# Routing tokens through DRAM to their two experts in a recurrent + mixture-of-experts kernel

## Chip, core and metric

One core of one Trainium2 chip runs the whole program. The metric is device time in microseconds of one launch, as the median of three runs.

## What is computed (reference, cut)

```python
# x: (2, 2048, 256) fp32; 4096 tokens
xB = einsum('bsd,nd->bsn', x, B)                    # n = 128 states
state = tanh(state @ A.T + xB[:, t])                # for t in 0..2047, in order
y = states @ C.T + D * x + x
x = layernorm(x + layernorm(y) * gamma + beta)
scores = sigmoid(x @ router_weight.T)               # 8 experts in 2 groups of 4
# choose the better group, in it the top 2 experts; weights normalised to sum 1
g, u = x @ w_gate[e], x @ w_up[e]                   # 256 -> 128, for each expert
routed = sum_e comb[t, e] * ((silu(g) * u) @ w_down[e])
shared = (silu(x @ sw_gate) * (x @ sw_up)) @ sw_down
out = layernorm(x + routed + shared)
```

Only two of the eight entries of `comb` are not zero for a token. The reference computes all eight experts.

## The kernel before, in words

The sequence is cut into 128 chunks of 32 tokens, one chunk to a partition; a tile `l` (0 to 31) holds the l-th token of every chunk. The scan therefore has 32 serial steps for all chunks together. A first pass of 4 + 32 steps (`WARM` = 4) finds the state at which each chunk starts; a second pass of 32 steps from these seeds writes `states`. At the end of the second pass `met` compares the seeds with the last states; if they differ by more than 2^-20, a serial path is taken. Each scan step is a `BT` product issued ahead (`drive`), an `AT` product (L298) and a tanh on ScalarE (L512).

While the first pass runs, x and the weights are loaded by SyncE. VectorE takes each weight's largest absolute value (L620), scales it and splits it in two fp16 halves, high and low (`split`, L647 and L649). An fp32 product is made of three fp16 products: high*high, high*low, low*high. GpSimd prepares `xskip` = x*(1+D) (L918, eight times) and x+beta (L926, eight times).

After the scan the tokens are worked in 8 groups of 4 tiles (512 tokens). For each group g all 9 experts (8 routed and the shared one) follow one another. For an expert: 12 fp16 products of 512 columns for gate and up (`up_products`, L371), a silu on ScalarE (L554), a product on VectorE (L827), for a routed expert a second one with its column of `comb` (L831), a high half on ScalarE (L565), a low half on GpSimd (L961), and 12 fp16 products of 256 columns for down (`down_product`, L439). The columns of `comb` are written to DRAM (L236) and read back spread over all partitions (L241, 8 loads of 256 KB a group).

Between the experts of group g, `piece(e, g + 1, ...)` does the front part of group g+1: C product (L333 or L338), statistics (L675, L680), gamma (L699), residual (L706), second normalisation (L715), transposes on TensorE (L348), their halves (L494, L721), logits (L359), and `choose` and `weigh` (L740 to L786). GpSimd does the inverse square roots (`rsqrt`, L942 and L944). The order on every engine is written out by hand in `group`; `Fori` loops over pairs of groups.

## Time and profile before

| | |
|---|---|
| median of 3 runs | 424.69 us (422.93 to 426.33) |
| profiled execution, span | 423.6 us |
| between its span and the median of the runs | 1.1 us |
| TensorE busy (matmul) | 378.8 us, 89% |
| VectorE busy | 323.5 us, 76% |
| GpSimd busy | 163.7 us, 39% |
| ScalarE busy | 138.0 us, 33% |
| DMA | 29.95 MB, 71 GB/s over the span |

The scan ends at 95.3 us, the groups' experts run from 98 to 416 us, and the rest is the last normalisation and the last store. A busy engine is not by itself the bound: which wait ends last in a stage has to be read there. Times are from the start of the span.

### The profile page before, as it was taken

To read this page: it belongs to the slowest core of one execution; us is meant where nothing else is said; L and a number is where in the kernel's file an instruction comes from. 1 tells how busy PE (TensorE), PEld (TensorE's weight loads), DVE (VectorE), ACT (ScalarE), POOL (GpSimd) and SP (SyncE) were. 2 spreads that over 40 slices of the span, in tenths; PEclk is the share of its full clock that TensorE was granted. 3 is DMA by queue.
4 is the path that set the end of the run, shared out by engine and by line. 5 is a ranking of instruction groups with operands and counts; after the bars stand their busy time and mean duration, and the time that the engine had idled before them with its cause. 6 is when DMAs were issued, how large, how long until landed. Compare 5 with 4: busy or idle time off the path is not lost.

```text
span 423.6 us, 7485 instructions
## 1 busy us (share of the span) xinstructions
PE 378.8 (89%) x2583; PEld 254.6 (60%) x2583; DVE 323.5 (76%) x740; ACT 138.0 (33%) x280; POOL 163.7 (39%) x151
## 2 busy tenths in 40 slices
PE   6899529596999998999899999999998999899992
PEld 5899428582566665666556556655565565565561
DVE  2343998445587699979978997999699969984464
ACT  2454102132233423242433244233432342333330
POOL 1870697300442334235423542344244234514242
PEclk9999958699899999999999999999999999999997
DMA  7980000003800460153018211901260145016311
GB/s 187 315 300 2 0 0 2 0 2 63 140 2 0 86 117 2 52 123 79 7 47 152 49 52 34 158 8 50 68 132 0 50 109 93 0 53 141 59 52 50
DMA packets 15901, 29.95 MB, mean 71 GB/s; under 512 B 1720, under 2 KB 4288, under 8 KB 15872
## 3 DMA queue, kind: packets, MB, share of 16 engines
q1 hardware_dynamic: 15872, 29.58, 29.9%
q8 instruction: 17, 0.28, 0.3%
q14 instruction: 12, 0.10, 0.1%
HBM read 25.24 MB, written 4.33 MB: 70 GB/s over the span
## 4 chain that ended last, share of the span: by engine, by line
issue 28%; PE 22%; POOL 18%; DVE 18%; DMA 5%; SPq 5%; ACT 2%; POOLq 1%; DVEq 0%; ACTq 0%
PE bank L371 11%; POOL h L961 9%; PE bank L439 4%; POOL xres L926 4%; DVE st L675 3%; SPq L205 3%; POOL rstd L944 3%; DVE wu L706 3%; DVE xT L827 3%; DMA xT<-comb_dram 2%; PE bank L292 2%; DVE xT L831 2%; DVE wg L715 2%; DMA xres<-in_L_attn_x_dram 2%; PE bank L298 1%
## 5 line engine op out<-in xcount | busy, mean ns | idle before, releaser
L961 POOL TENSOR_TENSOR h<-xT,h 128x512 f16<-128x512 f32 x72 | 86.2, 1198 | 185.8 <-ACT h L565 177.0
L439 PE MATMUL bank<-wd,h 128*128 128x256 f16 x864 | 106.9, 274 | 5.6 <-POOL h L961 4.9
L371 PE MATMUL bank<-x2T,wg 128*128 128x512 f16 x432 | 105.3, 379 | 0.0
L371 PE MATMUL bank<-x2T,wu 128*128 128x512 f16 x432 | 105.3, 379 | 0.0
L439 PEld LDWEIGHTS bank<-wd,h 128*128 128x128 f16 x864 | 84.4, 98 | 30.5 <-POOL h L961 5.7
L565 ACT ACTIVATE h<-xT 128x512 f16<-128x512 f32 x72 | 45.3, 630 | 131.7 <-DVE xT L831 128.2
L371 PEld LDWEIGHTS bank<-x2T,wu 128*128 128x128 f16 x432 | 42.3, 98 | 50.3
L827 DVE SCALAR_TENSOR_TENSOR xT<-bank,u_un,xT 128x512 f32<-128x512 f32 x64 | 47.6, 744 | 23.1 <-ACT xT L554 22.2
L554 ACT ACTIVATE xT<-bank,g_un 128x512 f32<-128x512 f32 x72 | 49.2, 683 | 43.2 <-PE bank L371 40.4
L371 PEld LDWEIGHTS bank<-x2T,wg 128*128 128x128 f16 x432 | 41.8, 98 | 35.6 <-issue 0.3
L831 DVE TENSOR_TENSOR xT<-xT 128x512 f32<-128x512 f32 x64 | 44.3, 692 | 8.4 <-DMA xT<-comb_dram 6.5
L292 PE MATMUL bank<-xT,BT 128*128 128x128 f32 x272 | 44.7, 290 | 0.0
L292 PEld LDWEIGHTS bank<-xT,BT 128*128 128x128 f32 x272 | 38.9, 206 | 0.1
L944 POOL TENSOR_TENSOR rstd<-rstd,neghalf 128x4 f32<-128x4 f32 (+1 forms) x25 | 25.6, 1025 | 2.0
L918 POOL TENSOR_TENSOR xskip<-xres,D_bc 128x1024 f32<-128x1024 f32 x8 | 20.5, 2586 | 10.3 <-issue 7.3
L675 DVE BATCH_NORM_STATS2 st<-wu 128x6 f32<-128x256 f32 x64 | 23.3, 416 | 0.8
L512 ACT ACTIVATE states<-bank 128x128 f32<-128x128 f32 x32 | 8.9, 278 | 42.2 <-PE bank L298 42.2
L706 DVE SCALAR_TENSOR_TENSOR wu<-wu,rstd,xres 128x256 f32<-128x256 f32 x32 | 21.7, 742 | 1.0 <-POOL rstd L944 1.0
L926 POOL TENSOR_TENSOR xres<-xres,beta_bc 128x1024 f32<-128x1024 f32 x8 | 22.3, 2815 | 0.0
L348 PE MATMUL bank<-ident,wg 128*128 128x128 f32 x64 | 11.2, 294 | 12.4 <-DVE wg L715 7.7
L715 DVE TENSOR_SCALAR wg<-wu,mv,rstd 128x256 f32<-128x256 f32 x32 | 19.7, 679 | 1.7 <-POOL rstd L944 1.4
L333 PE MATMUL bank<-CT,states 128*128 128x256 f32 x16 | 6.4, 516 | 13.0 <-DVE wu L690 13.0
(114 smaller groups left out, 356.8 us busy)
## 6 DMA issues: line engine op xcount, KB each, us to landing
xT<-comb_dram SPq DMA_DIRECT2D x64, 256.0 KB, 7.5
xres<-in_L_attn_x_dram SPq DMA_DIRECT2D x7, 512.0 KB, 5.9
out_dram<-xskip SPq DMA_DIRECT2D x7, 512.0 KB, 2.7
wd<-in_L_ffn_w_down_dram SPq DMA_DIRECT2D x1, 1024.0 KB, 7.0
xres<-in_L_attn_x_dram SPq DMA_DIRECT2D x2, 256.0 KB, 3.4
out_dram<-xskip SPq DMA_DIRECT2D x2, 256.0 KB, 2.0
B_sb<-in_L_attn_B_dram SPq DMA_DIRECT2D x1, 128.0 KB, 2.2
C_sb<-in_L_attn_C_dram SPq DMA_DIRECT2D x1, 128.0 KB
```

The lines of the kernel that those rows point to most:

```text
L292: pe.matmul(ps_scan[s % 2][:, 0:P], BT[:, k, :], xT[:, k, tile, :], start=(k == 0), stop=False)
L371: last = pe.matmul(ps[:, :], w[:, pw, e, m // 3, :], x2T[:, par, px, m // 3, :], start=(m == 0), stop=(m == NUP // 2 - 1))
L439: return pe.matmul(ps_y[t // 2][:, (t % 2) * DM:(t % 2 + 1) * DM], h16[:, e % 3, ph, t * P:(t + 1) * P], wd16[:, pw, e, :], start=start, s ...
L554: nc.scalar.activation(sg[:, b, :], ps_g[b][:, :], ACT.Silu, scale=g_un[:, 0:1]).then_inc(silu_done, 1)
L565: nc.scalar.activation(h16[:, e % 3, 0, :], h[:, b, :], ACT.Copy).then_inc(h_high, 1)
L675: nc.vector.bn_stats(st[:, k, t, :], src(t)).then_inc(st_sem, 1)
L706: nc.vector.scalar_tensor_tensor(y1[:, t, :], y1[:, t, :], rstd[:, 0, 1, t:t + 1], xres[:, g * T4 + t, :], ALU.mult, ALU.add).then_inc(sem ...
L827: nc.vector.scalar_tensor_tensor(gu[:, b, :], ps_u[b][:, :], u_un[:, 0:1], sg[:, b, :], ALU.mult, ALU.mult).then_inc(gu_done, 1)
L831: nc.vector.tensor_tensor(h[:, b, :], comb_all[:, e - 1, :], gu[:, b, :], ALU.mult).then_inc(h_done, 1)
L926: nc.gpsimd.tensor_tensor(xres[:, c * T4:(c + 1) * T4, :], xres[:, c * T4:(c + 1) * T4, :], beta_bc[:, :].unsqueeze(1).to_broadcast([P, T4 ...
L944: nc.gpsimd.tensor_tensor(rstd[:, k, 1, t0:t1], rstd[:, k, 0, t0:t1], neghalf[:, t0:t1], ALU.pow).then_inc(ready, 1)
L961: nc.gpsimd.tensor_tensor(h16[:, e % 3, 1, :], h[:, b, :], h16[:, e % 3, 0, :], ALU.subtract).then_inc(h_low, 1)
```

## The change

- The first scan pass has 32 steps instead of 36. Loads are reordered (the down weights last). The greatest weights are combined over partitions by two small TensorE steps instead of GpSimd. Only gate, up and router weights are split; `wd` and `C` stay fp32, and their products are single fp32 products.
- Normalised tokens are kept as fp16 high and low halves, one row of 1 KB for each token (`rows16`), and are transposed by TensorE as fp16.
- After the choice of experts (`choose`, now with `max` and `max_index` for each tile), TensorE ranks each token within its expert by products with a triangle and with ones (`ranks`), VectorE turns ranks into row numbers (`slots`), and GpSimd writes the rows to DRAM, sorted by expert, by 8 indirect DMAs of 128 rows for each group (`scatter`), 64 in all.
- The groups are in two parts, 0 to 4 and 5 to 7 (`PARTS`). At the end of a part `count`, `table` and `back` make lists of tiles of 256 rows, and SyncE fills the unused rows (`pad`, 9 DMAs). There are always 27 tiles in part 0 and 19 in part 1.
- A tile is one routed job: a DMA transpose of 256 rows of 1 KB from DRAM (`load_tile`), 12 fp16 products of 256 columns with the weights of an expert read from a table, silu, one product on VectorE, 2 fp32 products for down, a copy by ScalarE (`keep_y`) and a store to DRAM. 16 jobs of 256 tokens do the shared expert. That makes 62 jobs.
- At the end, for each pair of tiles u (16 pairs), GpSimd reads each token's two rows back by 4 indirect DMAs (`gather`), VectorE adds them with their weights (`combine`), GpSimd makes the inverse root (4 small instructions), and ScalarE normalises (`finish`). Pairs 0 to 9 belong to part 0 and stand between the routed jobs of part 1.
- The path for seeds that were not met is a serial one at the end of the program.
- The order on all engines comes from one list of tokens (`PLAN`), fully unrolled.

```diff
-    WARM = 4
+    PARTS = ((0, 5), (5, 8))
+    SLOTS = 2 * P
+    JT = [TK * (g1 - g0) * GT // SLOTS + E - 1 for g0, g1 in PARTS]
+    RING = 4
+    LAG = 2
+        def period(p, jobs, spread):       # p: group in front, g: group routed
+            g = p - 1
+            if p > 2:
+                if p < G:
+                    put(("A", p))
+                put(("X", g, 0), ("X", g, 1))
+                some(spread[0])
+                if p < G:
+                    put(("S", p))
+            put(("Y", g, 0), ("Y", g, 1))
...
+            put(("T", g, 0))
+            some(spread[1])
+            put(("T", g, 1))
+            if p > 2 and p < G:
+                put(("B", p))
+            some(spread[2])
...
+            put(("L", g))
+            some(spread[3])
+            put(("D", g))
+            some(spread[4])
+            put(("P", g))
+            some(spread[5])
+            put(("E", g))
+            if g + 1 == PARTS[part_of[g]][1]:
+                put(("N", part_of[g]))
...
+        period(5, shared(3), (0, 1, 0, 1, 0, 0))
+        period(6, shared(4) + shared(5)[:0] + ra[:5], (1, 1, 1, 1, 1, 2))
+        period(7, ra[5:13], (1, 2, 1, 2, 1, 1))
+        period(8, ra[13:20], (1, 1, 1, 2, 1, 1))
+        for what in ra[20:] + shared(5):
+            job(*what)
...
+            def load_tile(h, j):                                   # SyncE
+                row = sp.value_load(tabR[0:1, h, j:j + 1], min_val=0, max_val=E * CAP[h])
+                sp.dma_start_transpose(xjob[:, r % RING, :, :], xs_dram[h][bass.ds(row, SLOTS), :]).then_inc(xjob_in[r % RING], 16)
...
+            def up(n):                                             # TensorE
+                    pe.wait_ge(xjob_in[r % RING], 16 * (r // RING + 1))
+                    e = pe.value_load(tabE[0:1, p, j:j + 1], min_val=0, max_val=E)
...
+            def scatter(g):                                        # GpSimd
+                pool.wait_ge(slots_ready, g + 1)
+                pool.wait_ge(x2_low, 2 * g + 2)
+                for t in range(g * T4, (g + 1) * T4):
+                    for r in range(TK):
+                        nc.gpsimd.indirect_dma_start(out=xs_dram[hp], out_offset=...)
+            def gather(u):
+                if u >= 2:
+                    pool.wait_ge(comb_step, 4 * (u - 1))
+                for t in range(2):
+                    for r in range(TK):
+                        nc.gpsimd.indirect_dma_start(out=yback[:, u % 2, t, r, :], out_offset=None, in_=ys_dram[hp], ...)
```

In `PLAN` the letters are: A the C product and first statistics, S gamma, B residual and second statistics, X the second normalisation and high half, Y the low half, T transposes, L logits, D choice, P ranks, E slots and scatter, N the tables of a part, J a job, G gather, Z combine, R inverse root, W finish and store.

## Rows read from the trace of the kernel before

**Rows 1.** Stretch, us; busy of PE, PEld, DVE, ACT, POOL; clock, DMA share, GB/s.
```profile
98.50:415.50 317.00, 303.76 (x2037) 186.91 (x2036) 262.21 (x632) 108.16 (x178) 113.39 (x114) 0.99 0.31 66
183.00:223.07 40.07, 38.92 (x267) 24.09 (x266) 35.69 (x88) 13.86 (x23) 14.71 (x15) 1.00 0.26 67
```
**Rows 2.** The chain that ended last: some of TensorE's pieces (start, us, what).
```profile
109.13 1.71 PE bank L333 x4
...
127.72 2.59 PE bank L371 x12
130.31 1.31 PE bank L439 x12
```
**Rows 3.** Timeline of the scan (start, us, engine, line, [idle before, releaser]).
```profile
42.75 0.28 ACT L518 ACTIVATE seed<-bank 128x126 f32<-128x126 f32 x1 [0.58 <-PE bank L298]
...
60.95 1.22 PE L333 MATMUL bank<-CT,states 128*128 128x256 f32 x2 [13.02 <-DVE wu L690]
...
78.85 0.69 PE L348 MATMUL bank<-ident,wg 128*128 128x128 f32 x2 [4.67 <-DVE wg L715]
...
95.03 0.28 ACT L512 ACTIVATE states<-bank 128x128 f32<-128x128 f32 x1 [0.82 <-PE bank L298]
```
**Rows 4.** The chain from 38 to 68 us.
```profile
38.31 7.25 issue
45.55 4.20 POOL xskip L918
49.75 17.61 POOL xres L926 x6
```
**Rows 5.** VectorE's groups by line and shape (busy us, mean ns of one).
```profile
L690 DVE TENSOR_TENSOR wu<-bank,xskip 128x512 f32<-128x512 f32 x4 | 2.8, 688 | 2.8 <-PE bank L333 2.7
L675 DVE BATCH_NORM_STATS2 st<-wu 128x6 f32<-128x256 f32 x64 | 23.3, 416 | 0.8
L699 DVE SCALAR_TENSOR_TENSOR wu<-wu,mv,gamma_bc 128x256 f32<-128x256 f32 x32 | 16.7, 563 | 0.6
L706 DVE SCALAR_TENSOR_TENSOR wu<-wu,rstd,xres 128x256 f32<-128x256 f32 x32 | 21.7, 742 | 1.0 <-POOL rstd L944 1.0
L721 DVE SCALAR_TENSOR_TENSOR x2T<-bank,x2T 128x512 f16<-128x512 f32 x16 | 10.8, 674 | 8.0 <-ACT x2T L494 8.0
```
**Rows 6.** Timeline of one steady group on VectorE and GpSimd.
```profile
188.91 0.88 DVE L699 SCALAR_TENSOR_TENSOR wu<-wu,mv,gamma_bc 128x256 f32<-128x256 f32 x2
...
195.14 2.57 DVE L706 SCALAR_TENSOR_TENSOR wu<-wu,rstd,xres 128x256 f32<-128x256 f32 x4
...
197.74 1.41 DVE L675 BATCH_NORM_STATS2 st<-wu 128x6 f32<-128x256 f32 x4
...
212.63 0.18 DVE L740 TENSOR_SCALAR score<-th 128x32 f32<-128x32 f32 x1
...
215.03 0.19 DVE L756 TENSOR_TENSOR choice<-choice,mask 128x32 f32<-128x32 f32 x1
```
**Rows 7.** GpSimd's groups by line and shape.
```profile
L961 POOL TENSOR_TENSOR h<-xT,h 128x512 f16<-128x512 f32 x72 | 86.2, 1198 | 185.8 <-ACT h L565 177.0 <-issue 8.8
L944 POOL TENSOR_TENSOR rstd<-rstd,neghalf 128x4 f32<-128x4 f32 x23 | 24.2, 1051 | 1.8
L942 POOL TENSOR_TENSOR rstd<-mv,eps 128x4 f32<-128x4 f32 x23 | 6.3, 274 | 21.3 <-DVE mv L680 21.3
```
**Rows 8.** DMA: SyncE's issues in the timeline, and the list of issues (KB, us to landing).
```profile
101.14 6.66 SPq L241 DMA_DIRECT2D xT<-comb_dram  x8
139.94 0.33 SPq L236 DMA_DIRECT2D comb_dram<-combT  x1
...
xT<-comb_dram SPq DMA_DIRECT2D x64, 256.0 KB, 7.5
```
**Rows 9.** Timeline at the read of `met` into registers.
```profile
96.57 0.15 DVE L808 TENSOR_SCALAR met<-met_row 128x1 int32<-128x1 f32 x1 [0.55 <-POOL met_row L951]
97.69 0.69 ACT L554 ACTIVATE xT<-bank,g_un 128x512 f32<-128x512 f32 x1 [2.38 <-DVE met L808]
```
**Rows 10.** Timeline: one small VectorE instruction twice, and GpSimd beside the second.
```profile
90.76 0.17 DVE L749 TENSOR_TENSOR top<-both 128x8 f32<-128x8 f32 x1
...
213.27 1.15 POOL L961 TENSOR_TENSOR h<-xT,h 128x512 f16<-128x512 f32 x1 [2.91 <-ACT h L565]
...
213.37 1.08 DVE L749 TENSOR_TENSOR top<-both 128x8 f32<-128x8 f32 x1
```

More of the change, by code:

```diff
@@ L10 @@
 I32 = mybir.dt.int32
+U32 = mybir.dt.uint32
 AX_X = mybir.AxisListType.X
-RMAX = bass.bass_isa.ReduceOp.max
 P = 128
@@ L40, in ssm_moe_kernel, with routed_upto, shared_upto, routed_index @@
+    PLAN = plan()
+    NJ = len(JOBS)
+    routed_jobs = [n for n in range(NJ) if JOBS[n][0] == "r"]
+    def routed_upto(n):
+        return sum(1 for m in range(n + 1) if JOBS[m][0] == "r")
+    def shared_upto(n):
+        return n + 1 - routed_upto(n)
+    def routed_index(n):
+        return routed_upto(n) - 1
     with ExitStack() as ctx:
@@ new lines, in ssm_moe_kernel @@
+        base = sb("base", [P, 2, E])
+        lower = sb("lower", [P, E, E])
+        pick = sb("pick", [P, L, TK, E])
+        kept16 = sb("kept16", [P, L, E], F16)
+        place = sb("place", [P, T4, E])
+        picked = sb("picked", [P, T4, TK, E])
+        slot = sb("slot", [P, L, TK])
+        slot_i = sb("slot_i", [P, L, TK], I32)
+        back_i = sb("back_i", [P, L, TK], I32)
+        gate = sb("gate", [P, L, TK])
+        LT = max(g1 - g0 for g0, g1 in PARTS) * T4
+        wide = sb("wide", [P, LT, TK, E])
@@ L130, in ssm_moe_kernel @@
+        x_in = [sem(f"x_in{i}") for i in range(G)]
         x_rest = sem("x_rest")
@@ L404, in _ @@
-            for n in range(n_up, 2 * NUP):
-                early_up(n)
+                if s == WMAX_AT:
+                    pe.wait_ge(wmax_part, 3)
+                    pe.wait_ge(consts, 2)
+                    pe.transpose(ps_mats[0][0:3, 0:P], wmax[:, :], ident[:, :]).then_inc(wmax_turned, 1)
+                if s == WMAX_AT + 4:
+                    pe.wait_ge(wtop_done, 3)
+                    pe.matmul(ps_mats[0][:, P:P + 3], ones[:, :], wdiag[:, :], start=True, stop=True).then_inc(wmax_turned, 1)
@@ new lines, in _ @@
+            tables = 0
+            for token in PLAN:
+                kind, n = token[0], token[1]
+                if kind == "scan":
+                    scan_step(L + n, tiles, seeds if n == 0 else states[:, n - 1, :])
+                elif kind == "A":
+                    if n == 0:
+                        pe.wait_ge(Cr_done, 2)
+                    project(n)
+                elif kind == "T":
+                    turn_x2(n, token[2])
+                elif kind == "L":
+                    if n == 0:
+                        pe.wait_ge(weights_ready, 3)
+                    logits(n)
+                elif kind == "P":
+                    ranks(n)
+                elif kind == "N":
+                    count(n)
+                elif kind == "J":
+                    if n < NJ:
+                        if JOBS[n][0] == "r" and JOBS[n][2] == 0:
+                            pe.wait_ge(table_ready, JOBS[n][1] + 1)
+                        up(n)
+                    if 0 <= n - LAG < NJ:
+                        down(n - LAG)
@@ L410, in _ @@
             with pe.If(runs_met == 0):
+                pe.wait_ge(sl_in, 16 * G)
+                for l in range(L):
+                    pe.wait_ge(sl_cp, l + 1)
+                    for k in range(KT):
+                        last = pe.transpose(bank[2][:, k * P:(k + 1) * P], xres[:, l, k * P:(k + 1) * P], ident[:, :])
+                    last.then_inc(sl_tr, 1)
+                pe.wait_ge(sl_cp, L + 1)
                 with pe.Fori(0, NCH) as c:
@@ L469, in _ @@
[L469 to L484 removed]
+                pe.wait_ge(sl_w, 64)
```

1341 lines of the change are left out of this document (789 added, 552 removed).

## Prediction

> **What bounds the kernel now.** I read the busy times by stretch first. All groups together take 317 us with TensorE busy for 304, and a steady group of 40.07 us has 38.92 us of TensorE, 35.69 of VectorE and 14.71 of GpSimd [rows 1]. The chain of waits then says what one expert costs: 2.59 us for the twelve 512-column products and 1.31 us for the twelve 256-column ones [rows 2]. Nine times 3.90 is 35.1 us of the 40.07; the other 5 are the front part of the next group. So this stage is bound by TensorE, with VectorE close behind. The scan before it is not: its second pass starts from the seed at 43.0 and ends at 95.3, though a free step takes 0.85 us and 32 of them would take 27. It lost 13.0 us to the first addition on VectorE, which stood behind the weight splits, and 4.7 to the second normalisation [rows 3]; the chain under both is GpSimd's skip and residual work up to 67.4 us [rows 4].
>
> **What the change removes.** 72 expert passes of 3.90 us are 281 us of TensorE. In their place stand 62 jobs. A job's gate and up products have the shape count of the old down product, twelve of 256 columns, 1.31 us. Its two fp32 down products have the shape of the C product, 1.71/4 = 0.43 us each [rows 2]. That is 2.17 us a job and 135 us in all. If TensorE stayed the bound, 146 us would go. It does not, and the rest of the sum is about what comes late next.
>
> **Scan.** Four steps fewer are 3.4 us, so the second pass starts at about 39.5. The splits of down and C weights go, and VectorE is no longer late at 60 us. What is late next is GpSimd: ScalarE, which is in the scan's chain, now waits at step 17 for the second inverse root of group 0. GpSimd has eight skips, then three residuals instead of six before the first root. From the chain it ends its skips at 49.7 [rows 4]; with less blocking by splits I put that at 42 to 45. Three residuals at 2.9 us (17.61/6) end near 52, the first root near 54, one more residual and VectorE's four residual additions and statistics (2.6+1.4+0.5) lead to the second root near 61. Step 17 would be due at 39.5+14.8 = 54, so 6 us are lost. Fourteen more steps are 12 us, and ScalarE gets some 8 us of other work in between (four normalised pairs, two copies, one tanh), 3 us remain for transposes and waits. Scan end: 84 us (78 to 90) in place of 95.
>
> **Front part by group.** Now VectorE sets the pace, for a group's front part no longer hides under 35 us of experts. For one group: addition and statistics 2x0.69+1.41+0.5 = 3.3; gamma 4x0.44 = 1.8; residual and statistics 2.57+1.41+0.5 = 4.4; low half 2x0.67 = 1.4 [rows 5, 6]. I use the timeline's uncontended values, since the group means 563 and 742 ns hold GpSimd's share. The choice takes 2.6 us up to the mask [rows 6], and then eleven small steps with eight `max` and `max_index`, which no row shows; at 0.17 us each and one wait per batch I put 1.9, so 4.5 (3.5 to 7). Slots 0.9. Two shared jobs 2x(0.41+0.69) = 2.2. Sum 18.5 us. To it comes what VectorE waits for: the C product behind the ranks in TensorE's order, 1.0, and the ranks themselves, up to 20 tiny products, 1.2.
>
> GpSimd can make this longer. A group's eight indirect DMAs stand ahead of the next group's first root, which VectorE needs after 3.3+1+1.8+1.4+0.4 = 8 us. The root is now four instructions, 0.27x3+1.05 = 1.9 us [rows 7]. **The price of an indirect DMA on GpSimd is the number this forecast hangs on, and no row has it.** Below stands a plain DMA's issue on SyncE, 0.33 us, or 0.83 us apart when eight follow one another [rows 8]; above stand GpSimd's 128x1024 instructions at 2.9 us. It has to form 128 row addresses, and I take 1.2 us, what GpSimd takes for 128x512 elements [rows 7], the row nearest to work on all partitions. Then 9.6+1.9-8 = 3.5 us are lost. A group costs 18.5+2.2+3.5 = 24.2 us. Periods 3 to 5: 73 us. Period 2 has no C product but two choices and two scatters: 19 us of VectorE and 5 of waiting, 24.
>
> The trace shows the two engines in each other's way: the same VectorE instruction took 0.17 us alone and 1.08 us beside a GpSimd one [rows 10]. The Trainium skill (SBUF — State Buffer, the section on its two physically separate sides) says more: descriptors of a DMA issued from GpSimd are written through the port pair it shares with VectorE, so 0.62 us alone became 3.1 us beside a VectorE copy. By that price a scatter of eight would take 25 us and the 128 indirect DMAs 397 us; no run so far shows such a DMA.
>
> **Routed jobs.** Each has two reads of a table entry into a TensorE register. The nearest row is the read of `met`: from its end at 96.72 to ScalarE's start at 97.69, 0.97 us with a branch in it [rows 9]. Hidden behind queued products it costs nothing, exposed 1.9 us a job. I take 2.6 us a job (2.2 to 3.3). Period 6 has the tables on VectorE (22 small steps, about 5.8 us) and five routed jobs; 26.5 us of VectorE, some waits under cover: 28. Its first routed job comes 17 us in, and the rows are there at about that time: tables 3, nine pads at about 1 us with their register reads, the scatter meanwhile, then the load 4. Period 7: eight jobs, 21, and 4.4 of other products: 26. Period 8: seven jobs, 18, and 4: 22. Then seven routed and two shared jobs, 22.6, and 5 us in which TensorE waits, as SyncE's queue holds the second padding (9 us, and the wait for the last scatter) ahead of all but four of the loads and ahead of the stores of results.
>
> The transposing load of 256 KB is the second unknown. Eight plain 256 KB loads go out in 6.66 us and land 7.5 us after issue [rows 8], so about 1 us each, when they do not wait. A job every 2.6 us hides 1 to 2.6 us. I take it as hidden. It then costs nothing; without that cover every microsecond over 2.6 costs 46 us.
>
> The Trainium skill has two rules here that differ. Advanced Engine Details and Errata (X-Bar Transpose) says that such DMAs are as fast as plain ones; VectorE: DVE Perf Modes (The three transpose paths) gives 1309 ns for one 128x128 block. A job has eight blocks: by the first the load stays hidden, by the second a job's load would take 10.5 us and 46 of them 482 us. The trace before has no transposing DMA.
>
> **Combining.** From the last job of part 0, GpSimd has 16 pairs to serve: 4x1.2 for the gathers and about 1.6 for the four small instructions on two columns, 6.4 us. VectorE needs 4x0.5+0.75+0.33 = 3.1 us a pair and two jobs of part 1 need 5.2, so GpSimd is the slowest of the three throughout, and the part's 19 jobs (50 us) are over before the tenth pair (64 us). 2.5 us until the first rows land, 16x6.4 = 102, 5 for the last root, normalisation and store: 110 us.
>
> **Sum.** 84+24+73+28+26+22+22.6+5+110 = 395 us of span. The profiled span was 423.6 and the median 1.1 above it; 396 us.
>
> **Rivals.**
> First, faster: an indirect DMA costs 0.5 us of GpSimd. Nothing is lost behind scatters, a group costs 20.7 us, the jobs 2.2. Then 84+20+62+25+22+19+20+19x2.5+4x2.2+6x3.6+5 = 335 us, up to 360 with slower jobs. For it: SyncE's issue of 0.33; against: GpSimd's smallest instructions already take 0.27, and 1.05 for a power of four columns [rows 7].
>
> Second, slower: GpSimd's DMAs cost more than 1.5 us each. Each tenth of a microsecond adds 16x0.4 = 6.4 us at the end and 0.8 us in each of some five groups, 10 us in all. It decides from 1.5 us, where the time is 426; at 1.9 us it is 466. For it: the collisions of the two engines [rows 10] and the skips stretched from 2.4 to 4.2 us [rows 4].
>
> Third, slower: the loads are the bound. They start at about 185 us, and 46 of them at T us each are followed by 9 us of shared jobs and 43 us of the last six pairs. With 185+46T+52 the mark is T = 4.1 us; at 6 us it is 513. For it: SyncE is one queue, which holds a register read, a load and a store for each job. Against: what plain loads do [rows 8].
>
> Fourth, that the change does not do what it says: if the seeds are not met, 2048 serial steps of 0.85 us are added, 1.7 ms and more. From the reference in double precision the largest difference is 2.3e-7 after 32 steps and 2.7e-7 after 36, against 9.5e-7; it should be met as before.
>
> **Chances.** The forecast with its neighbours (365 to 420) has 0.47, the faster rival 0.21, GpSimd's price 0.15, the loads 0.13, the serial path 0.02, other 0.02. A measurement of this kernel can tell about 1% from no change (its runs spread over 0.8%). Faster by over 1%, under 420.4: 0.47+0.21 less the upper edge, 0.65. Within 1%: 0.07. Slower: 0.28. The range is 345 to 470: it leaves out the fastest part of the first rival and the slow ends of the others. The forecast's own range is 365 to 420.
>
> **What the profile after would show.** TensorE busy for about 190 us instead of 379; scan end near 84; about 24 us from one scatter to the next; an indirect DMA of 1.2 us on GpSimd and GpSimd's rows at the head of the last 110 us of the chain; TensorE waiting for no load but the first of each part. I am wrong if a gather takes under 0.8 or over 1.5 us, if TensorE's longest waits are on the transposed loads, if `max` and `max_index` make the choice longer than 7 us, or if TensorE, busy for a third of the time between 84 and 181 us, is granted the lower clock so often that its short steps get on VectorE's path.

## The result, and the profile after

The changed kernel takes 453.96 us (median of 4, 450.65 to 455.07) beside 424.79 for the kernel before on the same chip: 1.068 times as long, 95% interval 1.063 to 1.074. The forecast of 396 us had the wrong sign. The profiled execution has a span of 453.3 us.

First the page's busy times and slices of the changed kernel, then stretches in the columns of [rows 1]: the front part of groups 1 to 4, the stretch in which tokens are sorted and most routed jobs run, the first ten pairs of the combining, and the last six.

```profile
PE 276.1 (61%) x1951; PEld 218.4 (48%) x1951; DVE 229.6 (51%) x753; ACT 140.1 (31%) x306; POOL 219.1 (48%) x293
...
PE   6899978255537375248799483769577776350000
...
ACT  2464244240222223013455331223142424311110
POOL 2995351367646454510813306000677767357761
PEclk9899989666677676789899799769889989695555
```
```profile
98.50:182.00 83.50, 46.96 (x340) 35.22 (x340) 56.29 (x226) 21.38 (x37) 47.91 (x61) 0.70 0.15 54
...
182.00:316.50 134.50, 94.16 (x685) 73.10 (x686) 57.22 (x219) 43.28 (x80) 34.98 (x44) 0.87 0.66 178
316.50:396.00 79.50, 51.74 (x298) 34.99 (x296) 35.69 (x100) 26.92 (x57) 53.78 (x80) 0.89 0.85 204
400.00:445.00 45.00, 2.65 (x12) 1.66 (x10) 19.25 (x54) 5.65 (x11) 32.74 (x48) 0.59 0.33 99
```

TensorE was busy for 0.96 of the stretch of experts in [rows 1]; now no engine is busy for more than 0.73 of any stretch. Where no engine is busy throughout, the time lies in the order in which the engines wait for each other, and there the 58 us have to be looked for that the forecast lacks.

GpSimd's two groups of indirect DMAs, the number on which the forecast hung (columns as in [rows 7]):

```profile
L1252 POOL DMA_INDIRECT xs_dram<-xres,slot_i x64 | 65.1, 1018 | 82.0 <-DVE slot_i L971 64.7
L1267 POOL DMA_INDIRECT yback<-ys_dram,back_i x64 | 66.4, 1038 | 62.4 <-DMA ys_dram<-wu 41.0
```

1.02 and 1.04 us busy; from one start to the next it is 1.28 in a row of stores and 1.30 in a row of gathers. The next lines are from the timeline of period 8:

```profile
247.25 0.61 PE L532 MATMUL bank<-ident,xres 128*128 128x128 f16 x8
247.47 0.47 ACT L747 ACTIVATE sg<-bank,g_un 128x256 f32<-128x256 f32 x1
...
248.96 0.97 POOL L1252 DMA_INDIRECT xs_dram<-xres,slot_i  x1 [0.30 <-issue]
...
252.77 0.97 POOL L1252 DMA_INDIRECT xs_dram<-xres,slot_i  x1 [0.30 <-issue]
255.34 1.02 ACT L733 ACTIVATE xT<-bank 128x1024 f16<-128x1024 f16 x1 [7.41 <-remote]
...
257.25 0.48 DVE L1044 SCALAR_TENSOR_TENSOR h<-bank,u_un,sg 128x256 f32<-128x256 f32 x1 [8.80 <-ACT sg L747]
```

ScalarE's instruction at 255.34 copies the transposes that TensorE ended at 247.86. For 7.41 us it stands, and "remote" says that no event in the trace released it; VectorE waits 8.80 us and TensorE 5.91 behind it. GpSimd's row of eight stores began at 243.72 and ended at 253.74. Such waits end at 117.58 (6.50 us) and 226.09 (3.99) too, 2.1 and 0.6 us behind a row's end, and at 221.63 (2.67) inside a row. The trace of before has no such wait on ScalarE.

The releaser that a line names is inferred, so the kernel has to be read beside it. This copy waits in the program for the transposes alone, and a silu for its own up product and for VectorE's product two jobs before. By that measure one more silu stands still, though its line names a releaser:

```profile
274.69 0.82 PE L597 MATMUL bank<-xjob,wu 128*128 128x256 f16 x6
...
282.88 0.47 ACT L747 ACTIVATE sg<-bank,g_un 128x256 f32<-128x256 f32 x1 [8.35 <-DVE h L1044]
```

Its up product ended at 275.51 and ScalarE's instruction before it at 274.53; the product of VectorE that ended at 282.85 is that of the job before, for which the program does not make it wait. It stands for 7.4 us, up to the end of group 7's row of eight at 282.89. The brackets are idle time and can hold more than the standing still: the silu at 117.58 has had its up product since 112.58, so 5.0 of its 6.50 us. A wait for code is not the reason. In this trace the packets that load instructions start at 104.13 and 139.08, at 215.21 and 232.02, at 244.10 and 263.20 with none between, around the stalls that end at 117.58, 221.63 and 226.09, and 255.34.

Two more waits, each with the line that shows it: SyncE's zero fills of part 0 and the first routed job behind them, and the gathers of the first and of the eleventh pair behind the last store of their part's results.

```profile
181.93 10.44 SPq L399 DMA_DIRECT2D xs_dram<-zeros  x8
...
195.85 5.21 SPq L391 DMA_TRANSPOSE xjob<-xs_dram  x3
```
```profile
200.17 1.46 PE L597 MATMUL bank<-xjob,wg 128*128 128x256 f16 x6 [5.79 <-issue]
...
316.52 1.07 POOL L1267 DMA_INDIRECT yback<-ys_dram,back_i  x1 [33.62 <-DMA ys_dram<-wu]
...
399.87 1.07 POOL L1267 DMA_INDIRECT yback<-ys_dram,back_i  x1 [7.38 <-DMA ys_dram<-wu]
```

A pair of the last six, with no job beside it:

```profile
412.17 1.29 POOL L1267 DMA_INDIRECT yback<-ys_dram,back_i  x1 [0.52 <-issue]
...
413.76 1.01 POOL L1267 DMA_INDIRECT yback<-ys_dram,back_i  x1 [0.30 <-issue]
...
415.08 1.00 POOL L1267 DMA_INDIRECT yback<-ys_dram,back_i  x1 [0.31 <-DVE mv L1073]
416.39 0.99 POOL L1267 DMA_INDIRECT yback<-ys_dram,back_i  x1 [0.30 <-issue]
417.40 0.21 POOL L1239 TENSOR_TENSOR rstd<-mv,eps 128x2 f32<-128x2 f32 x1
...
419.34 1.27 POOL L1267 DMA_INDIRECT yback<-ys_dram,back_i  x1 [0.52 <-issue]
```

GpSimd's instructions stand one behind the other with no wait of any size: it sets these pairs, 7.17 us each.

### The profile page after: what moved, and what is told of

The parts are those of the page before. It is cut to its first block, busy times and chain, and to the rows that moved or that the text cites. A ratio compares the mean times of both kernels' runs of the same rounds, so it can differ in the third digit from the quotient of the medians.

```text
span 453.3 us, 6946 instructions
## 1 busy us (share of the span) xinstructions
PE 276.1 (61%) x1951; PEld 218.4 (48%) x1951; DVE 229.6 (51%) x753; ACT 140.1 (31%) x306; POOL 219.1 (48%) x293
## 4 chain that ended last, share of the span: by engine, by line
issue 48%; POOL 13%; PE 12%; SPq 9%; DMA 7%; DVE 5%; ACT 2%; another core or an unknown queue 2%; POOLq 0%; ACTq 0%; DVEq 0%
POOL yback L1267 9%; PE bank L597 7%; PE bank L616 4%; DMA yback<-ys_dram,back_i 3%; SPq L362 3%; POOL rstd L1242 2%; SPq L398 2%; SPq L399 2%; DVE xskip L1066 2%; DMA xjob<-xs_dram 1%; DMA xs_dram<-zeros 1%; DMA ys_dram<-wu 1%; SPq L357 1%; DVE st L1070 1%
## 5 line engine op out<-in xcount | busy, mean ns | idle before, releaser
L1252 POOL DMA_INDIRECT xs_dram<-xres,slot_i x64 | 65.1, 1018 | 82.0 <-DVE slot_i L971 64.7
L1267 POOL DMA_INDIRECT yback<-ys_dram,back_i x64 | 66.4, 1038 | 62.4 <-DMA ys_dram<-wu 41.0
L616 PE MATMUL bank<-wd,h 128*128 (+1 forms) x248 | 73.7, 424 | 16.4 <-issue 9.3
L1044 DVE SCALAR_TENSOR_TENSOR h<-bank,u_un,sg 128x256 f32<-128x256 f32 x62 | 29.4, 475 | 80.9 <-ACT sg L747 76.6
L616 PEld LDWEIGHTS bank<-wd,h 128*128 128x128 f32 x248 | 47.0, 210 | 32.2 <-issue 26.3
L597 PE MATMUL bank<-xjob,wg 128*128 128x256 f16 x276 | 42.2, 294 | 28.7 <-DVE h L1044 14.4
L747 ACT ACTIVATE sg<-bank,g_un 128x256 f32<-128x256 f32 x62 | 29.2, 472 | 75.0 <-PE bank L597 57.5
L1066 DVE SCALAR_TENSOR_TENSOR xskip<-yback,gate,xskip 128x256 f32<-128x256 f32 x64 | 28.1, 481 | 38.6 <-DMA yback<-ys_dram,back_i 38.0
L597 PEld LDWEIGHTS bank<-xjob,wg 128*128 x276 | 26.1, 104 | 42.3 <-issue 36.3
L760 ACT ACTIVATE xskip<-xskip,rstd 128x256 f32<-128x256 f32 x32 | 17.5, 593 | 88.7 <-POOL rstd L1244 88.7
L597 PE MATMUL bank<-xjob,wu 128*128 128x256 f16 x276 | 42.3, 295 | 0.0
L754 ACT ACTIVATE wu<-bank 128x512 f32<-128x512 f32 x46 | 27.1, 590 | 18.6 <-PE bank L616 13.7
L597 PEld LDWEIGHTS bank<-xjob,wu 128*128 x276 | 29.2, 106 | 5.3
L532 PEld LDWEIGHTS bank<-ident,xres 128*128 128x128 f16 x128 | 10.8, 121 | 35.4 <-issue 17.5
```

Source lines behind the costliest of these rows:

```text
L532: last = pe.transpose(x2_turn[:, a, k, t * P:(t + 1) * P], rows16[:, g * T4 + 2 * half + t, a, k * P:(k + 1) * P], ident16[:, :])
L597: last = pe.matmul(ps_gu[n % 2][:, i * SLOTS:(i + 1) * SLOTS], weights(w, pw, k), cols[:, px, k, :], start=(m == 0), stop=(m == 3 * KT - 1))
L616: last = pe.matmul(ps_y[n % 2][:, t * DM:(t + 1) * DM], h[:, n % 3, t * P:(t + 1) * P], rhs, start=True, stop=True)
L747: nc.scalar.activation(sg[:, n % 2, :], ps_gu[n % 2][:, 0:SLOTS], ACT.Silu, scale=g_un[:, 0:1]).then_inc(silu_done, 1)
L754: nc.scalar.activation(ysb[:, r % 4, :, :], ps_y[n % 2][:, :].rearrange("p (t d) -> p t d", t=2), ACT.Copy).then_inc(y_kept, 1)
L1044: stt(h[:, n % 3, :], ps_gu[n % 2][:, SLOTS:2 * SLOTS], u_un[:, 0:1], sg[:, n % 2, :], ALU.mult, ALU.mult).then_inc(h_done, 1)
```

## Experiments

Each starts from the changed kernel unless it says otherwise. "First gather" is where the combining begins in the profiled run, "rest" is what follows until the end of the span; between them they tell which half an edit reached. The ratio is to the kernel before, timed beside it (423.8 to 425.3 us). The edits are shown cut.

| kernel | median us | ratio (95%) | first gather | rest |
|---|---|---|---|---|
| changed kernel | 453.96 | 1.068 (1.063 to 1.074) | 316.5 | 136.8 |
| e1 half the gathers | 437.09 | 1.025 (1.017 to 1.033) | 316.9 | 118.1 |
| e2 early fill | 439.59 | 1.035 (1.030 to 1.040) | 302.4 | 136.1 |
| e3 three jobs a pair | 468.14 | 1.102 (1.096 to 1.109) | 315.9 | 150.0 |
| e4 plain loads | 451.33 | 1.062 (1.058 to 1.066) | 316.2 | 134.6 |
| e5 late half | 440.7 (one run) | | 302.2 | 136.7 |
| e6 short root | 455.45 | 1.074 (1.067 to 1.081) | 319.6 | 135.2 |
| e7 jobs first | 452.29 | 1.068 (1.062 to 1.073) | 319.2 | 128.9 |
| e8 | 433.48 | 1.024 (1.018 to 1.029) | 303.9 | 127.8 |
| e9 late scaling | 455.23 | 1.071 (1.067 to 1.075) | 319.5 | 133.6 |
| e10 plain stores | 415.20 | 0.977 (0.973 to 0.981) | 276.3 | 135.2 |
| e11 five edits | 414.14 | 0.975 (0.971 to 0.980) | 286.7 | 124.3 |
| e12 even parts | 425.56 | 1.002 (0.998 to 1.007) | 280.7 | 143.4 |
| e13 quarters | 410.67 | 0.966 (0.959 to 0.973) | 283.1 | 125.4 |
| e14 paused | 447.32 | 1.056 (1.051 to 1.060) | 309.7 | 136.0 |

**e1, half the gathers.**

```diff
-                for t in range(2): for r in range(TK):   # gather
+                for t in range(2): for r in range(1):
-  stt(xskip[...], yback[:, par, t, r, :], gate[...], ...)
+  stt(xskip[...], yback[:, par, t, 0, :], gate[...], ...)
```

> Leaves out the gathers of the second choice (32 of 64 indirect DMAs; the second product then reads the rows of the first choice). Theory A (GpSimd's issue of indirect DMAs sets a pair of the combining: 4 x 1.30 us of the 7.0): a pair falls to 4.4 us in the last six pairs (-16 us), and in the first ten to the 5.2 us of its two routed jobs (-18 us); in all 420 us, 415 to 428. Theory B (the pairs are paced by the landing of the DMAs or by VectorE's combining, and GpSimd only waits with them): the pair stays at 6.5 us or more, over 440 us.

Measured 437, between the two theories' times, so theory A named the right engine for half of it only. The last pairs start at 403.27, 407.61, 412.41 and 417.14, some 4.6 us apart, as it said. In the first ten they start every 6.8 us, though GpSimd now waits in each. The timeline of this kernel shows a ring there:

```profile
341.92 1.79 DVE L1066 SCALAR_TENSOR_TENSOR xskip<-yback,gate,xskip 128x256 f32<-128x256 f32 x4
...
344.93 0.19 POOL L1239 TENSOR_TENSOR rstd<-mv,eps 128x2 f32<-128x2 f32 x1 [2.52 <-DVE mv L1073]
...
346.38 1.09 ACT L760 ACTIVATE xskip<-xskip,rstd 128x256 f32<-128x256 f32 x2 [3.71 <-POOL rstd L1244]
...
347.85 0.46 ACT L747 ACTIVATE sg<-bank,g_un 128x256 f32<-128x256 f32 x1
...
348.34 0.48 DVE L1044 SCALAR_TENSOR_TENSOR h<-bank,u_un,sg 128x256 f32<-128x256 f32 x1 [3.20 <-issue]
...
348.75 1.79 DVE L1066 SCALAR_TENSOR_TENSOR xskip<-yback,gate,xskip 128x256 f32<-128x256 f32 x4
```

VectorE's combining, GpSimd's root, ScalarE's scaling, the silu that stands behind the scaling, the product that stands before the next combining: 348.75 - 341.92 = 6.83 us round. GpSimd's queue (7.1) and this ring (6.8) are near each other, so that taking work from either alone gives little.

**e2, early fill.** The rows are this input's.

```diff
-    for e in range(E):                      # pad(h), after the last scatter
-        row = sp.value_load(fill_i[0:1, h, e:e + 1], ...)
-        sp.dma_start(xs_dram[h][bass.ds(row, SLOTS), :]..., zeros[:, :])
+    for row in [e * CAP[h] + SLOTS * FILL[h][e] for e in range(E)] + [E * CAP[h]]:
+        sp.dma_start(xs_dram[h][row:row + SLOTS, :]..., zeros[:, :])   # in the scan
+    pool.wait_ge(padded[hp], 16 * (E + 1))  # scatter(g)
```

> The 18 zero fills go out in the scan, at fixed rows that fit the expert counts of this input, so that no value is read and nothing is sent between a part's last scatter and its first load. Theory A (the 10 us of fills on SP's queue hold up loads and stores behind them, and TensorE with them): the first routed job starts some 8 us earlier, the wait for the second part's first rows goes, and the first gather starts 10 to 18 us earlier: 438 us, 430 to 446. Theory B (what is late before the first gather is VectorE with its tables and the groups' own waits, and the fills lie beside it): 448 us or more.

439.6 us, the first gather 14.1 us earlier, what follows it as long: theory A. The scatter of group 5 starts at 207.4 in place of 214.5, and from the scatter of group 7 to the first gather it is 36.2 us in place of 43.6.

**e3, three jobs a pair.**

```diff
-            if j >= 1 and j % 2 == 1 and u <= nu:
+            if j >= 2 and j % 3 == 2 and u <= nu:
                 combine(u, 0, nu)
```

> Part 1's 19 routed jobs stand three to a pair of part 0 in the order of work, not two. Theory A (these jobs are paced by the pairs through VectorE's written order, which puts a pair's combining ahead of the next product): the jobs are over 3 to 4 pairs before the last pair of part 0, their stores with them, so that the 7.4 us wait of the eleventh pair's gather goes; pairs stay at 7.0 to 7.8 us: 447 us, 442 to 451. Theory B (the jobs need the time themselves, 7 us for two, by loads or DMA engines): pairs become 10 us long in this stretch and the total stays within 2 us of the changed kernel or over it.

14 us slower, where theory A had 7 faster. The numbers of theory B hold: the six steps that carry three jobs are over by 371.41, and behind the first of them the pairs are 7.6 to 12.0 us long, 10.0 in the mean, where they are 7.3 in the changed kernel at the same places. That alone is the 14 us. Its reason, loads or DMA engines, is not shown; the jobs also lie in the ring above. Why the wait of the eleventh pair did not go, as theory A had it, is in the order of work: a job's down product, copy and store stand one to three places behind its own, and after the last routed job there are no such places until the leftover pairs are through. The timeline of this kernel:

```profile
379.01 26.62 SPq L434 DMA_DIRECT2D out_dram<-xskip  x5
...
403.03 1.46 PE L597 MATMUL bank<-xT,wg 128*128 128x256 f16 x6 [28.39 <-DVE h L1044]
...
405.78 4.11 SPq L428 DMA_DIRECT2D ys_dram<-wu  x3
...
412.55 1.08 POOL L1267 DMA_INDIRECT yback<-ys_dram,back_i  x1 [8.41 <-DMA ys_dram<-wu]
```

TensorE stands for 28 us, the last three results go out at 405.8, and the eleventh pair waits for them: 19.8 us from the tenth pair, 18.6 in the changed kernel.

**e4, plain loads.**

```diff
-  sp.dma_start_transpose(xjob[:, r % RING, :, :], xs_dram[h][bass.ds(row, SLOTS), :])
+  sp.dma_start(xjob[:, r % RING, :, :], xs_dram[h][bass.ds(row, SLOTS), :].rearrange(...))
```

> The 46 transposing loads are plain loads of the same 256 KB (so that tokens and channels stand in the wrong places, and the outputs are other numbers). Theory A (order and GpSimd set the time; loads land 3.2 us after issue and are three jobs ahead): 448 to 455 us. Theory C (the loads are the limit, with DMA engines at 0.8 to 1.1 busy from 300 us on, and gathers and stores wait behind their small packets): SP's issue falls from 1.24 us to 0.5, pairs get shorter by 1 us or more, the wait of 33.6 us before the first gather shrinks; 435 us or less.

451.3 us, as theory A said. SyncE's issue of a load falls from 1.24 us to 0.34 and the time by 2.6, which the intervals do not tell from nothing. ScalarE's stalls stay, 5.6 us in the place of the 7.4. The third rival is out.

**e5, late half.**

```diff
+            if (g - 1) + 1 not in [g1 for _, g1 in PARTS]:
+                put(("E2", g - 1))        # behind ("L", g)
-                for t in range(g * T4, (g + 1) * T4):      # scatter(g)
+                for t in range(g * T4 + t0, g * T4 + t1):  # 0 to 2 at E, 2 to 4 at E2
+                    pool.wait_ge(logits_done, g + 2)       # at E2
```

> The indirect stores of a group's third and fourth tile wait for the next group's logits, some 15 us later; nothing else moves. In five traces so far ScalarE stands still with nothing that it waits for, and starts 0 to 2 us after GpSimd's last indirect store (253.7 and 255.3 us, for one). Theory S (ScalarE can't go on while GpSimd's row of indirect DMAs runs): the stall of 7.4 us in period 8 is cut to 3 us or less and another of up to 5 us comes up at the second half. Theory P (the stall belongs to that place of ScalarE's program, whatever GpSimd does): it stays 5 to 8 us long, at the same two instructions. The total stays within 5 us of the changed kernel by either.

The stall of period 8 is gone and 3.0 us are left of those of period 7 (the one at group 7's unbroken row stays: 10.1 us idle, 9.2 of them behind its up product), as theory S said, and the first gather comes 14.3 us earlier; "within 5 us" was a miss. Most of the 14.3 is not the stalls of periods 7 and 8: the scatter of group 4 already starts at 166.1 in place of 176.3. From group 2 to 4 the periods are 21.0 and 20.6 us in place of 24.4 and 22.5, and the changed kernel has no stall there. Four stores fewer stand on GpSimd ahead of the next group's inverse root, which is the term of 3.5 us a group that the forecast had. This is one run; e11, which holds the same edit, has 21.0 and 20.7 us there.

**e6, short root.**

```diff
+  ts(rstd3[:, par, 0, :], mv3[:, par, :, 1], LN_EPS, None, ALU.add).then_inc(mv3_ready, 1)   # VectorE
+  ts(rstd3[:, par, 2, :], mv3[:, par, :, 0], -1.0, None, ALU.mult).then_inc(mv3_ready, 1)
-  rsqrt(mv3_done, ...)                                  # GpSimd: four instructions
+  nc.gpsimd.tensor_tensor(..., ALU.pow); nc.gpsimd.tensor_tensor(..., ALU.mult)
```

> Two of GpSimd's four small operations for a pair's last root (variance plus a constant, minus the mean) go to VectorE. Theory A (GpSimd's queue is what sets a pair where no job runs): the last six pairs fall from 7.15 to 6.6 us (-3.3 us). For the first ten: if GpSimd sets them too, they fall as well, 8 to 9 us in all, 445 us; if the ring that half the gathers left at 6.8 us sets them (VectorE's combining, GpSimd's root, ScalarE's scaling, then silu and the product that wait behind it), it gets 0.1 us shorter at best, and the total is 449 to 452 us.

The last six pairs are 6.7 us long, as expected; the first ten go from 7.4 to 7.2 in the mean, so GpSimd does not set those alone. The total is over both forecasts. The first gather came 3.1 us later than in the changed kernel though nothing ahead of it was touched (e7 and e9, untouched there too, have 2.7 and 3.0; e1, e3 and e4 were within 0.6). So this front part scatters by 3 us from one set of runs to another, and the rest is compared and not the total.

**e7, jobs first.**

```diff
-        for j, what in enumerate(rb):
+        for j, what in enumerate(rb + shared(6) + shared(7)):
             job(*what)
-            if j >= 1 and j % 2 == 1 and u <= nu:
+            if (j % 2 == 1 and j < 18) or j == 21:
                 combine(u, 0, L // 2)
```

> The last routed job, and the four shared jobs of groups 6 and 7, stand ahead of the last pair of part 0, and the pairs run on without a break from part 0 to part 1. Theory A' (what the three-jobs order showed: the store of the last routed job stands three places behind its job, and those places came only behind the leftover pairs): the 7.4 us wait of the eleventh pair's first gather goes, with the 3.4 us gap of the pair before it; 443 to 447 us. Theory B (the wait is that of the jobs' own length): it moves to the tenth pair and the total stays within 3 us of the changed kernel.

The gap before the eleventh pair went from 18.6 us to 10.6, and the rest is 7.9 us shorter, as theory A' had it. The median shows only 1.7 of it, the figure of theory B: the front part took 2.7 us of the gain, and the profiled run, 449.9 us, is the fastest of four.

**e8** is e2, e6 and e7 with VectorE's table one job later:

```diff
-                elif kind == "N": table(n); back(n)
+                elif kind == "N": todo = [(table, n), (back, n)]
                 elif kind == "J":
+                    if todo: what, of = todo.pop(0); what(of)
```

> Fills in the scan, short root and jobs first together, and VectorE's table of a part one job later, its way back two jobs later (so that products don't queue behind 6 us of small operations). If the parts add up: 454 - 14 - 9 - 4 to 9 - up to 4 = 418 to 427 us, the time of the kernel before within 1.5 %. If they cover one another (the fills' gain is lost in VectorE's or GpSimd's wait before the first gather): 430 us or more.

433.5 us, where 418 to 427 was the sum. The parts are there as measured alone (the first gather of e2 within 1.5 us, the rest of e7 within 1.1), so they do not cover one another; they were worth less than I had put in. The later table brought nothing: from group 7's scatter to the first gather it is 36.8 us, in e2 36.2. TensorE waits as long as before, 6.78 us at 280.67, now for a silu that stands beside group 7's row of stores; in e2 the same stall lies beside the table:

```profile
278.80 0.47 ACT L744 ACTIVATE sg<-bank,g_un 128x256 f32<-128x256 f32 x1 [9.91 <-remote]
```

**e9, late scaling**, with e6 in it:

```diff
-                put(("Z", u - 1), ("R", u - 1), ("W", u - 1))
+                put(("Z", u - 1), ("R", u - 1))
+                held.append(("W", u - 1))   # put behind the next job
```

> The short root, and ScalarE's scaling of a pair (with its store) one job later in the written order. Ring theory (the first ten pairs are set by VectorE's combining, GpSimd's root, ScalarE's scaling, and the silu and product queued behind it, 6.8 us round): without the 1.1 us of scaling the ring is 5.7 us, GpSimd's 6.6 sets the pair, and the ten pairs get 0.5 us shorter each: 450 us beside the short root's 455.5. GpSimd theory (it set them already): within 1.5 us of the short root alone.

No gain over e6, the time that the GpSimd theory gave. Pairs without a stall are 6.5 to 6.8 us, beside 6.6 to 6.9 in e6, so the run hardly parts the two theories; and four ScalarE waits marked "remote", of 2.7 to 3.8 us, have come up among the gathers, 12.3 us in all, which e6 does not have there. The ring is thus shown by e1 alone.

**e10, plain stores.**

```diff
-  nc.gpsimd.indirect_dma_start(out=xs_dram[hp], out_offset=...(ap=slot_i[:, t, r:r + 1]), in_=...)
+  nc.gpsimd.dma_start(xs_dram[hp][to:to + P, :], ...)
```

> The indirect stores of the sorting are as many plain stores of the same 128 KB from GpSimd's queue to fixed rows, and every row that a job may load is filled with zeros in the scan (rows hold other tokens than they should, or zeros). If ScalarE's stalls hang on the making of the indirect stores' 128 addresses each, they go, and the time falls by some 20 to 28 us (14 for the fills, 8 to 13 for the stalls): 425 to 434 us. If they hang on DMAs from GpSimd's queue as such, they stay: 438 us or more.

415 us, 10 under the lower end of what was expected, and ScalarE's group has no "remote" in it:

```profile
L748 ACT ACTIVATE sg<-bank,g_un 128x256 f32<-128x256 f32 x62 | 29.2, 472 | 57.6 <-PE bank L598 54.4 <-issue 3.1
```
```profile
120.80 4.32 POOL L1255 DMA_DIRECT2D xs_dram<-xres  x8 [5.53 <-issue]
140.03 4.33 POOL L1255 DMA_DIRECT2D xs_dram<-xres  x8 [4.89 <-issue]
159.05 4.33 POOL L1255 DMA_DIRECT2D xs_dram<-xres  x8 [6.05 <-issue]
```

Eight plain stores take 4.3 us of GpSimd where eight indirect ones take 10, and a period is 19.1 us where it was 22.5 and 24.4. Beside e2 the first gather comes 26.1 us earlier. 17.5 of these are there when group 4's scatter starts, in periods whose only stall in e2 is the 6.39 us that end at 117.26; they are in the main GpSimd's own time ahead of the next root. The other 8.6 come behind it, where the stalls were. None is left beside the stores, so they hang on the indirect stores and not on GpSimd's queue as such. In the first row of gathers, which are still indirect, one silu stands 2.7 us behind its up product (at 283.58, marked "issue").

**e11, five edits**: e5, e2, e6, e7 and e9's late scaling.

> Late second half of the stores, fills in the scan, short root, jobs first, late scaling, together. Sum of the parts: 454 - 13 (late half) - 14 (fills) - 8 (the part behind the first gather, of short root and jobs first) - 5 (late scaling) = 414 us. If the fills' gain and the late half's are the same wait before the first gather seen twice: 424 to 428 us.

414.1 us, and 2.5% under the kernel before. It is the sum that was forecast, in part by luck: of the 5 us put in for the late scaling e9 had shown none. "Remote" waits of 16.9 us in all are left on ScalarE.

**e12, even parts**: e11 with

```diff
-    PARTS = ((0, 5), (5, 8))
+    PARTS = ((0, 4), (4, 8))       # and routed jobs from period 5 on, three to a pair behind period 8
```

> As the kernel with all five edits, and the parts are 4 and 4 groups, so that part 0 is combined from the end of the last group on, three jobs to a pair. Theory A (what is left after the last job is GpSimd's pairs, 6.6 us each, and GpSimd stood idle 80 us before the first gather): the first gather starts some 20 to 25 us earlier, eight pairs lie beside 27 jobs of 2.8 to 3.1 us, and eight follow: 402 us, 395 to 412. Theory B (the middle is bound by jobs that only move from one side of the last group to the other): 414 us or more, no gain over the uneven parts.

11 us slower than e11, where theory A had 12 faster. The first gather comes only 6 us earlier; with three jobs to a pair it is 7.7 to 9.6 us long; and the second half of one scatter and the whole of the next run on as 12 indirect stores from 140.8 to 156.1. The longest idle time of ScalarE marked "remote" in any run is behind them, of which it stood 7.4 us with its up product there since 150.45:

```profile
157.90 0.47 ACT L753 ACTIVATE sg<-bank,g_un 128x256 f32<-128x256 f32 x1 [14.26 <-remote]
```

**e13, quarters**: e11 with the stores two by two (`("E2", g - 1, 1, 2)` behind Y, `2, 3` behind T, `3, 4` behind L).

> As the kernel with all five edits (414 us), and a group's indirect stores go out two by two (from period 3 on, at the next group's low parts, transposes and logits; the two last groups of the parts still in one row of eight). Theory R (ScalarE stands still only from about the fifth indirect DMA of a row on): the halves left little to gain there, the stall behind group 6's half, 2.9 us, goes, and the total is 409 to 414 us. Theory N (every indirect DMA costs ScalarE a share, whatever its place): stalls stay as long in sum, 414 us or more.

410.7 us, inside theory R's range and 3.4% under the kernel before; its interval overlaps that of e11. No "remote" is left on ScalarE, nor a silu or copy of the transposes that starts over 0.5 us later than the program lets it.

**e14, paused.**

```diff
+                    if g >= 5 and t == g * T4 + 1:     # between the fourth and the fifth store
+                        for k in range(2):
+                            nc.gpsimd.tensor_tensor(pause[:, :, :], D_bc..., gamma_bc..., ALU.mult)
```

> In the changed kernel the rows of eight indirect stores of groups 5 to 7 have a pause of about 3.6 us of ordinary GpSimd work between the fourth and the fifth (nothing else moves; a group's stores end 3.6 us later). Theory R (a row must be unbroken to hold ScalarE up): the stalls of periods 7, 8 and of the last store shrink from 4 to 9 us each to 3 or less, and the first gather starts 5 to 12 us earlier: 442 to 450 us. Theory N (ScalarE waits until a group's eight are through, however they are spread): stalls get 3 us longer each and the total is 456 to 464 us.

447.3 us: GpSimd does more, each of these rows takes 3.6 us longer, and the kernel is 6.6 us faster. The same place as above, in this kernel:

```profile
247.64 1.03 POOL L1254 DMA_INDIRECT xs_dram<-xres,slot_i  x1 [0.30 <-issue]
247.85 1.03 ACT L735 ACTIVATE xT<-bank 128x1024 f16<-128x1024 f16 x1
248.69 3.72 POOL L1260 TENSOR_TENSOR pause<-D_bc,gamma_bc 128x768 f32<-128x768 f32 x2
...
251.03 1.02 ACT L735 ACTIVATE xT<-bank 128x1024 f16<-128x1024 f16 x1 [1.30 <-PE bank L534]
...
252.56 1.01 POOL L1254 DMA_INDIRECT xs_dram<-xres,slot_i  x1
```

ScalarE goes on at 247.85 with the copy that stood until 255.34. From group 6's scatter to group 7's it is 21.9 us in place of 29.2.

## Why the prediction was wrong

| step | forecast | measured |
|---|---|---|
| scan end | 84 | 81.3 |
| period of a group, 3 to 5 | 24.2 | 24.4, 22.5 |
| choice of experts | 4.5 | 3.7 |
| first routed job | 198 | 200.2 |
| indirect DMA on GpSimd | 1.2 (0.8 to 1.5) | 1.28 to 1.30 |
| scatters of groups 4, 5, 6, 7 | 181, 209, 235, 257 | 176.3, 214.5, 243.7, 272.9 |
| first gather | 284.6 | 316.5 |
| combining to the end | 110 | 136.8 |

The engine named was right, GpSimd, and so was its price, nearly: 0.1 us more an indirect DMA is about 10 us by the forecast's own sensitivity. Up to the scatter of group 4 the sum was 4.7 us long, and its term for the stores ahead of the next root is borne out by e5. Two steps failed.

**"some waits under cover: 28", "Period 7: eight jobs, 21, and 4.4 of other products", period 8 and the "seven routed and two shared jobs, 22.6, and 5 us in which TensorE waits".** These four terms give 103.6 us from the scatter of group 4 to the first gather; it is 140.2. The stretches in the kernels that take something away:

| us, from the first store of | forecast | changed | e14 | e2 | e13 | e10 |
|---|---|---|---|---|---|---|
| group 4 to group 5 | 28 | 38.1 | 36.2 | 30.9 | 31.7 | 31.2 |
| group 5 to group 6 | 26 | 29.3 | 31.7 | 29.4 | 29.8 | 29.9 |
| group 6 to group 7 | 22 | 29.2 | 21.9 | 29.4 | 22.8 | 22.5 |
| group 7 to first gather | 27.6 | 43.6 | 44.0 | 36.2 | 35.6 | 33.6 |

The fills cost 14 us (e2: 7.2 in the first stretch, 7.4 in the last) where the sum had 5 us for those of part 1 and took those of part 0 as covered, and that could have been seen: the forecast itself counted nine pads of 1 us on SyncE ahead of loads and stores, twice (measured: 10.44 us for eight, then the first load 3.0 us after the last, and TensorE's waits of 5.79 at 200.17 and 5.49 at 298.12). The stall of ScalarE cost 7 us, in the third stretch: there the forecast's 22 holds in all three kernels that have no stall at this place. The working priced TensorE's products and counted GpSimd's stores as lying beside them; while most of these rows of indirect stores run ScalarE stands, and with it, through the silu, VectorE's product and TensorE. No row of the trace before could show it. ScalarE's lines have 21.6 us of "remote" before the first gather, but idle time on one engine is not time of the kernel, and the stall at group 7 lies beside VectorE's tables and costs next to nothing by itself. About 16 us are left in e13, with neither fills nor stalls: a job takes 2.95 us (silus at 266.66 and 272.56, two jobs apart) where 2.6 was put in, and the tables on VectorE hold a product back, so that TensorE waits 6.66 us at 283.64 in the changed kernel and 4.95 in e13. How the rest divides was not tested. With fills and indirect stores out of the way (e10) the first gather comes at 276.3, 8 us ahead of the 284.6 of the sum, but only because its group 4 is 22 us ahead.

**"16x6.4 = 102", and "the part's 19 jobs (50 us) are over before the tenth pair".** A pair is 7.2 us where GpSimd is alone with it, 0.4 from the gathers' pitch and the rest from the gaps between its small instructions (1.94 from the root's start to the next gather, 1.6 forecast). In the first ten pairs it is 7.4 in the mean, with the ring of e1 close under GpSimd. The jobs are not free to run ahead: VectorE's written order has a combining behind every second product, so the jobs take as long as the pairs, and the last one's store comes only behind the tenth pair. The forecast compared three sums, GpSimd's, VectorE's and TensorE's, and took the largest; the ring goes through three engines and belongs to none of the sums. The gap between the tenth and eleventh pair, 18.6 us where 6.4 were forecast, is 12 of the 27 us; e7 gave back 8 of them.

The rivals: GpSimd's price decides "from 1.5 us", and it stayed under that, so the kernel became slower by another mechanism than the slower rival's. The loads were not the bound (e4). The seeds were met, so the serial path did not run. The wait for the first rows of part 1 was the only long one on a load, as said. Of the Trainium skill's three prices that the prediction weighed, the one of the shared port pair (SBUF — State Buffer, the section on its two separate sides), by which eight stores would take 25 us, is not met here: a gather beside VectorE's statistics takes 1.01 us (413.76 in the timeline), one beside its combining at most 1.29 (412.17). The page's figure is for a DMA beside a VectorE copy, and no VectorE copy of that length ran beside an indirect DMA here. The 1309 ns for a block (the Trainium skill, VectorE: DVE Perf Modes, The three transpose paths), by estimate 10.5 us a load, is not borne out. "As fast as plain" (the Trainium skill, Advanced Engine Details and Errata, X-Bar Transpose) holds for the total within 2.6 us. A load was issued at 294.01 and its first product ran at 298.12, which bounds its landing at 4.1 us.

TensorE's busy time was forecast at 190 us and is 276. Six products of 256 columns take 0.82 us at a granted clock of 1.00 (244.4 to 247.0). Behind waits of 5.5 to 6.7 us they take 1.46, at 0.50 (283.64 to 286.30 and 298.12 to 301.00), which is the lower level, 1.2 GHz. The granted clock is 0.87 over the stretch of jobs and 0.59 from 400 to 445. The sum had this as a risk and not as a term.

**Left open.** What a row of indirect DMAs and ScalarE share was not found. The changed kernel and e1, e4, e6 and e7 stall at nearly the same instructions (at 114 to 118, 226 to 228 and 255 to 258 us). e4 excludes the transposed loads' small packets, e10 GpSimd's queue, e14 the number of stores in a group, and the packets that load instructions a wait for code. An unbroken row does not always do it: in e14 the first sixteen stores (93.75 to 114.5) have no pause, and a silu and a copy run beside them without standing (110.32 and 112.53). e13's rows of eight at group 7 and at the first gathers show less than it seems, for ScalarE had nothing ready from their fifth and sixth DMA on. And e9's stalls in rows of four gathers show that the length of the row is not all of it either.

## What to carry to other kernels

Where no engine is the bound, price the written order and not the sums: walk once round each ring of engines (here combining, root, scaling, silu, product) and compare its length with the slowest engine's. Break up rows of indirect DMAs, two or four at a time with other work between, even if each group of them then ends later: here that took them from ahead of the next inverse root (e5) and took ScalarE's stalls away (e13, e14). A trace tells of such a stall by a wait that nothing releases, or by one whose named releaser the program does not wait for. And give no experiment's whole gain to one cause before the stretches are compared one by one: of e5's 14 us, 10 were not the stall that it was made for. And when a software pipeline ends, look for what stands one to three places behind the last item: its store may be queued behind everything that was only meant to fill in.

## What the runs showed of the hardware

- An indirect DMA of 128 rows of 1 KB costs GpSimd 1.02 us busy and 1.28 from start to start when it stores to DRAM, 1.04 and 1.30 when it gathers from it; a plain store of the same size 0.55 busy (e10).
- During unbroken rows of eight to sixteen indirect stores ScalarE stood still for up to 9.2 us (e5) with nothing in the program to wait for, mostly until 0 to 2 us after the row's end, but not in every such row. There is no such wait beside plain stores (e10), and a pause of 3.7 us after the fourth took those of periods 7 and 8 away (e14). The cause is open.
- 256 KB loads with a transpose cost SyncE 1.24 us each to issue, plain ones 0.34; the kernel with 46 plain ones was 2.6 us faster, which the intervals do not tell from nothing (e4).
- Eight zero fills with a register read each took SyncE 10.44 us in all, 1.3 us each.
